# Experts' layer of a fused four-layer kernel: four sets of tile buffers, one buffer for two norms, and a new order of the pieces

## The reference, cut to what matters

```python
q = jnp.einsum('btd,ed->bte', hidden_states, W_q)
sim = jnp.einsum('pbthn,hkpn->pbthk', q, keys)            # 2 x 4 heads x 64 keys
scores_xy, idx_xy = jax.lax.top_k(sim, K)                 # K = 8
all_scores = (sx[..., :, None] + sy[..., None, :]).reshape(b, t, h, K * K)
all_idx = (ix[..., :, None] * nk + iy[..., None, :]).reshape(b, t, h, K * K)
scores, pk = jax.lax.top_k(all_scores, K)
indices = jnp.take_along_axis(all_idx, pk, axis=-1)
w = jax.nn.silu(jnp.einsum('btd,bthkd->bthk', hidden_states, down_embed[indices])
                * jax.nn.softmax(scores, axis=-1))
experts_states = jnp.einsum('bthk,bthkd->btd', w, up_embed[indices])
dense = jnp.einsum('bti,di->btd', jax.nn.silu(jnp.einsum('btd,id->bti', hidden_states, W_up)), W_down)
return dense + experts_states
```

## Time and profile before

| quantity | value |
|---|---|
| median of three runs | 4945.19 us (4938.97 to 4951.75) |
| the profiled execution, its own time | 4949.86 us |
| its span | 4948.5 us |
| experts' layer, from fence to fence | 444.9 to 1078.4 us, 633.5 us |
| busy in its steady part, 513.0 to 1000.7 us | PE 283.4, DVE 406.4, ACT 389.1, POOL 419.0 us of 487.7 |
| first and last `xr` | 551.4 and 1077.7 us |

### The profile page before, as it was taken

How to read it: one execution, slowest core, us unless ns; L and a number is a source line. 1 busy time by engine, 2 the same in 40 slices (tenths; PEclk the granted TensorE clock), 3 DMA queues, 4 the chain that set the end, 5 groups by cost and what they waited for, 6 DMA issues and landing times.

```text
span 4948.5 us, 126756 instructions
## 1 busy us (share of the span) xinstructions
PE 4337.9 (88%) x51520; PEld 3291.1 (67%) x51520; DVE 3905.0 (79%) x6375; ACT 3256.5 (66%) x5035; POOL 3775.0 (76%) x2624
## 2 busy tenths in 40 slices
PE   7885565558867999999999999999999999999997
PEld 5664444446645677777777777777777777777776
DVE  4665888845548888888888888888888888888884
ACT  4664787754434677667676777667676677767675
POOL 1113888853448988888988898889888899888994
PEclk9998778779988999999999999999999999999999
DMA  2000000000001222222222222222222222222222
GB/s 60 2 2 1 1 1 1 1 25 2 2 1 34 52 49 51 66 50 55 51 58 59 56 50 50 63 54 56 50 59 53 53 53 52 62 52 55 49 55 56
DMA packets 120784, 197.93 MB, mean 40 GB/s; under 512 B 66896, under 2 KB 78224, under 8 KB 120080
## 3 DMA queue, kind: packets, MB, share of 16 engines
q1 hardware_dynamic: 120208, 189.82, 15.5%
HBM read 24.12 MB, written 2.10 MB: 5 GB/s over the span
## 4 chain that ended last, share of the span: by engine, by line
PE 65%; ACT 13%; POOL 6%; DVE 6%; issue 5%; DMA 4%; SPq 1%; ACTq 0%; POOLq 0%; DVEq 0%
PE ps L1299 8%; PE ps L1256 7%; PE ps L1249 7%; PE ps L1250 7%; DMA arena<-arena 4%; PE ps L1284 4%; PE ps L1290 3%; PE ps L1291 3%; PE ps L1351 3%; PE ps L1274 3%; PE ps L1310 3%; PE ps L1340 2%; ACT L1385 2%; PE ps L1334 2%; DVE arena L598 2%
## 5 line engine op out<-in xcount | busy, mean ns | idle before, releaser
L1574 POOL TENSOR_TENSOR arena<-arena 128x1024 f32<-128x1024 f32 x384 | 909.5, 2369 | 268.1 <-DVE arena L1474 267.7
L1569 POOL TENSOR_TENSOR arena<-arena 128x32 f32<-128x32 f32 x192 | 1045.0, 5443 | 0.1
L1473 DVE TENSOR_TENSOR arena<-ps,arena 128x1024 f32<-128x1024 f32 x384 | 470.2, 1225 | 344.9 <-ACT arena L1369 344.9
L1369 ACT ACTIVATE arena<-ps 128x1024 f32<-128x1024 f32 x384 | 393.0, 1024 | 386.3 <-PE ps L1250 381.7
L1592 POOL TENSOR_TENSOR arena<-arena 128x1536 f32<-128x1536 f32 x192 | 529.2, 2756 | 113.5 <-DVE arena L1507 113.5
L208 POOL TENSOR_SCALAR arena<-arena 128x2 f32<-128x2 f32 x256 | 87.5, 342 | 624.3 <-DVE arena L202 614.1
L1299 PE MATMUL ps<-arena 96*64 96x64 f32 x12288 | 419.2, 227 | 61.6 <-DMA arena<-arena 59.4
L1474 DVE TENSOR_TENSOR arena<-ps,arena 128x1024 f32<-128x1024 f32 x384 | 466.1, 1214 | 0.0
L1299 PEld LDWEIGHTS ps<-arena 96*64 96x64 f32 x12288 | 393.4, 140 | 91.9 <-issue 84.2
L1256 PEld LDWEIGHTS ps<-arena 128*128 128x128 f32 x3072 | 353.6, 144 | 150.8 <-issue 100.8
L1256 PE MATMUL ps<-arena 128*128 128x128 f32 x3072 | 419.4, 281 | 34.9 <-POOL arena L1579 33.9
(11 more groups left out here) (252 smaller groups left out, 10226.8 us busy)
## 6 DMA issues: line engine op xcount, KB each, us to landing
arena<-arena SPq DMA_DIRECT2D x192, 384.0 KB, 4.3
arena<-arena SPq DMA_DIRECT2D x192, 256.0 KB, 3.7
arena<-arena SPq DMA_DIRECT2D x192, 128.0 KB, 2.3
arena<-in_dWqkv SPq DMA_DIRECT2D x18, 512.0 KB, 3.6
arena<-arena SPq DMA_DIRECT2D x96, 64.0 KB
arena<-arena SPq DMA_DIRECT2D x96, 63.5 KB
arena<-in_dWo SPq DMA_DIRECT2D x6, 512.0 KB, 4.7
arena<-in_x SPq DMA_DIRECT2D x4, 512.0 KB, 7.5
```

The lines of the kernel that those rows point to most:

```text
L1473: dve.tensor_tensor(o1, p.rearrange("p (h e) -> p h e", h=16), bc(cs, 1, 16), ALU.mult)
L1569: pool.tensor_tensor(ss[:, 0:32], ss[:, 32:64], mhalf32, ALU.pow).then_inc(*S.rs.up())
L1574: pool.tensor_tensor(a1[:, half], a1[:, half], T2[:, half], ALU.add).then_inc(*radd[g].up())
```

## The change

- `Tile` exists four times. Batch b uses the sets `2 * (b % 2)` and `2 * (b % 2) + 1`, so a set is written again two batches later. Every wait for the last reader in a tile's buffer changes from the batch before (`if b >= 1: ... at(b)`) to the one before that (`if b >= 2: ... at(b - 1)`).
- `y` is gone. `n1` writes the normed output over `U.h`, and so waits for `h(b)` (which has read it), and `xr` adds `U.h`. Whoever writes `U.h` next is `n0` of three batches later: it waited for `h(b-3)` before and now waits for `xr(b-3)`. What `n1` waited for before (`xr(b-3)`) is dropped.
- `PLACE` has new numbers. Below are its first lines before and after.

```diff
-    Batch = namedtuple("Batch", "st nb h hT up y")
+    Batch = namedtuple("Batch", "st nb h hT up")
...
-                  sb([128, 4, 128])) for _ in range(2)]
+                  sb([128, 4, 128])) for _ in range(4)]
...
-    PLACE = {"n0": 0, "st0": 45, "r0": 54, "hT": 120, "spcA": 193, "piA": 301, "C1A": 370, "mxA": 384, "ixA": 430,
+    PLACE = {"st0": 0, "n0": 38, "hT": 189, "spcA": 304, "spcB": 377, "r0": 416, "piA": 417, "mxA": 511, "h": 521,
...
-            T = tiles[t]
+            T = tiles[2 * (b % 2) + t]
...
             if piece == "n0":
                 X, rs = XR[:, 2 * b:2 * b + 2, :], U.st[2]
                 if b >= NU:
-                    act.wait_ge(*S.h_ps.at(b - NU + 1))
+                    act.wait_ge(*S.xr.at(b - NU + 1))
                 act.wait_ge(*S.r0.at(b + 1))
...
             if piece == "n1":
-                if b >= NU:
-                    act.wait_ge(*S.xr.at(b - NU + 1))
+                act.wait_ge(*S.h_ps.at(b + 1))
                 act.wait_ge(*S.r1.at(b + 1))
                 p, rs = ps("ot", b), U.st[2]
-                act.activation(U.y[:, 0, :], p[:, 0:128], ACT.Identity, bias=U.nb[:, 0:1], scale=rs[:, 0:1])
+                act.activation(U.h[:, 0, :], p[:, 0:128], ACT.Identity, bias=U.nb[:, 0:1], scale=rs[:, 0:1])
...
             if piece in ("spcA", "spcB"):
-                if b >= 1:
-                    act.wait_ge(*gp[t].at(b))
-                    act.wait_ge(*pb[t].at(b))
+                if b >= 2:
+                    act.wait_ge(*gp[t].at(b - 1))
+                    act.wait_ge(*pb[t].at(b - 1))
...
-                pool.tensor_tensor(X, X, U.y, ALU.add).then_inc(*S.xr.up())
+                pool.tensor_tensor(X, X, U.h, ALU.add).then_inc(*S.xr.up())
```

More of the change, by code:

```diff
@@ L781, in phase_b @@
     NU = 3
-    Batch = namedtuple("Batch", "st nb h hT up y")
-    batches = [Batch(stats(C), sb([128, 2]), sb([128, 2, 128]), sb([128, 256]), sb([128, 4, 256]), sb([128, 2, 128]))
+    Batch = namedtuple("Batch", "st nb h hT up")
+    batches = [Batch(stats(C), sb([128, 2]), sb([128, 2, 128]), sb([128, 256]), sb([128, 4, 256]))
                for _ in range(NU)]
@@ new lines, in phase_b @@
+    PLACE = {"st0": 0, "n0": 38, "hT": 189, "spcA": 304, "spcB": 377, "r0": 416, "piA": 417, "mxA": 511, "h": 521,
+             "ixA": 523, "c8A": 576, "mxB": 582, "spA": 595, "mrA": 597, "C1A": 599, "ixB": 632, "C1B": 646,
+             "MA": 705, "nnA": 716, "c8B": 741, "ohA": 796, "mrB": 827, "eqA": 842, "piB": 863, "upc": 865,
+             "trA": 894, "spB": 898, "pcA": 909, "onA": 913, "paA": 922, "paB": 933, "xpA": 940, "txA": 953,
+             "thA": 1012, "xpB": 1014, "eqB": 1178, "pcB": 1227, "mkA": 1229, "up": 1234, "zzB": 1240, "geA": 1249,
+             "nnB": 1295, "trB": 1298, "zzA": 1331, "txB": 1393, "ohB": 1400, "MB": 1407, "sg0A": 1411, "sMA": 1425,
+             "onB": 1438, "pbA": 1461, "gpA": 1472, "sg1A": 1520, "thB": 1521, "mkB": 1596, "pbB": 1603, "geB": 1603,
+             "sg2A": 1646, "sg3A": 1647, "sg0B": 1679, "gpB": 1724, "sg1B": 2016, "atcA": 2103, "sg2B": 2213,
+             "sMB": 2295, "lsA": 2337, "sg3B": 2341, "atcB": 2470, "atA": 2494, "lsB": 2559, "st1": 2823, "n1": 2867,
+             "atB": 3155, "r1": 3250, "xr": 3453, "ot": 3459}
@@ L827, in batch @@
         def batch(piece, b):
-            U, T2 = batches[b % NU], tiles
+            U, T2 = batches[b % NU], (tiles[2 * (b % 2)], tiles[2 * (b % 2) + 1])
             if piece == "h":
@@ L858, in tile @@
         def tile(piece, b, t):
-            U, T = batches[b % NU], tiles[t]
+            U, T = batches[b % NU], tiles[2 * (b % 2) + t]
             if piece in ("spA", "spB"):
@@ L929, in tile @@
             if piece in ("piA", "piB"):
-                if b >= 1:
-                    act.wait_ge(*eq[t].at(b))
-                    act.wait_ge(*pb[t].at(b))
+                if b >= 2:
+                    act.wait_ge(*eq[t].at(b - 1))
+                    act.wait_ge(*pb[t].at(b - 1))
                 act.wait_ge(*ix[t].at(b + 1))
@@ L989, in tile @@
         def tile(piece, b, t):
-            T = tiles[t]
+            T = tiles[2 * (b % 2) + t]
             SIM, PRJ, ey, ex, e8, eC = views(T)
             if piece in ("mxA", "mxB"):
[L993 to L996, removed]
+                if b >= 2:
+                    dve.wait_ge(*pa[t].at(b - 1))
+                    dve.wait_ge(*C1[t].at(b - 1))
+                    dve.wait_ge(*ix[t].at(b - 1))
                 dve.wait_ge(*spc[t].at(b + 1))
```

70 lines of the change are left out of this document (35 added, 35 removed).

## The result

The changed kernel takes 4968.35 us (median of six runs, 4964.66 to 4977.12) against 4942.85 for the kernel before (six runs): ratio 1.0051, 95% interval 1.0040 to 1.0062, so 25 us slower. The forecast was 30 us slower, with a turn (from one `xr` to the next) of 39.8 us.

A forecast was written before the change was run, and what follows sets the result against it. Bound: a chain of data and order waits, no full engine. Four stretches, 19.3 + 10.2 + 3.3 + 7.0 = 39.8 us a turn, +2.3 over 13 batches, +30: 4980 against the profiled execution, median 4975 us, range 4922 to 5008.

The forecast's parts named there:

- What bounds the kernel before: Phase of 633.5 us: a chain of data and order waits through `r1` and `r0`, 37.52 us a turn; more buffers alone remove nothing.
- The loop through the new wait: `n0(b)` waits for `xr(b-3)`, behind `onB` and `nnB`; `mxA` follows: turn 39.8 us for 37.5, +2.3, met by 13 batches.
- Stretch 3: From the start of `nnB` to the end of `xr`, with POOL held by `tr`: 3.3 us, 2.0 from below.
- Stretch 4: From `xr` to `mxA`, through `n0`, `spA` and `spcA`, with PE slow after idling: 7.0 us, 5.3 from below.
- Stretches 1 and 2: DVE from `mxA(b)` to `st0(b+1)`, 19.3 us; then `st0(b+1)` to `nnB(b)`, 10.2 us, with `mkA` waiting for `txA` behind `r1`.
- the wait of 0.6 us for `txB`: Inside `mxA` to `st0`: `mkB` waits for `txB` behind `spB`, `spcB` and the table load, adding 0.6 us to 18.7.
- the end of the phase, set to nothing: Filling and draining of the phase: taken as nothing, give or take 8 us.
- The faster case: Order pays: `r1` ends within 1 us of `st0`, PE at full clock at `spA`; turn 34.4, 4905 us; chance 0.22.
- half-way case: Half of the faster rival's gain: turn 36.3 us or so, time 4930 us; within that rival's chance of 0.22.
- The case of the common ports as the bound: What POOL and DVE exclude each other from sets the turn: within 0.5 us, time within 7 of 4945; chance 0.14.
- the slower rival: `r0` late by one wide piece, so `gpA` holds `xr`: `nnB` to `xr` grows 2.3, turn 42.1, 5005 us; chance 0.14.
- The signs named beforehand: Turn near 40 us, `n0` waiting for `xr`, DVE idle before `mxA`, `mkA` waiting for `txA`, `xr` over 1 us, other phases unchanged.

The follow-up runs named there:

- two kernels that open it in different ways: Changed kernel with the output norm's separate buffer and earlier waits restored: 4915.41 us, ratio 0.9942; changed kernel with `xr` ahead of `r0` on POOL: 4927.19 us, 0.9965.
- the run with four sets: Changed kernel with four sets of statistics buffers in place of three, so `st0(b)` waits for `n1(b-4)`: 4979.74 us, ratio 1.0071.
- the own buffer: Changed kernel, but the output norm has its own buffer in unused `XX`, with the waits of before; same order and tile sets: 4915.41 us, ratio 0.9942.
- the two last kernels with the own buffer: Output norm's separate buffer in the changed kernel, plus four statistics sets and `n1` behind `xpB`: 4915.56 us; or three sets and `r1` ahead of `paA`: 4918.03 us.

## Why the prediction was right, point by point

**What bounds the kernel before:** confirmed in the part that was tried. More buffers in the old order changed nothing (0.9993), and the new order without the new wait shortened the turn to 34.8 us. That the old turn of 37.5 goes through `r1` and `r0` as the chain has it wasn't tried by a run.

**The loop through the new wait:** confirmed by two kernels that open it in different ways, at -4.1 and -3.3 us a turn. The prediction had DVE idle behind `gpA` right, but gave no figure for what the order would be worth without the wait. It is worth 0.58% of 4947, 29 us, and the wait costs the difference of the two ratios, 1.09%, 54 us, PE's lower clock in the changed kernel included.

**Stretch 3,** `nnB` to the end of `xr`: 3.3 us forecast, 744.80 - 741.54 = 3.26 measured. The rows of the trace before held the same sequence, 3.24 us long, and it repeated to within 0.02.

**Stretch 4,** `xr` to `mxA`: 7.0 forecast, 752.05 - 744.80 = 7.25 measured. PE was slow at `spA`, 3.78 us at a granted clock of 0.50, as it had been after idling in the earlier trace rows, where the clock from 733.0 to 737.3 was 0.56. The term matters: in all thirteen turns `spA` took 3.46 to 3.78 us, and after the one of 3.46 the next `n0` came after 38.71 us for 39.03 after the one shown. With the 1.98 us of the fast turns above, this turn would be 37.2 us by estimate (38.95 - 1.80), no longer than before the change, where `spA` is slow too.

**Stretches 1 and 2** were wrong apart and nearly right together. The forecast was 19.3 from `mxA` to `st0` and 10.2 from `st0` to `nnB`, with a wait of 3.6 us for `txA` in the second. Measured are 774.31 - 752.05 = 22.26 and 741.54 - 735.27 = 6.27: 28.5 for 29.5. The same wait for `r1(b-2)` stands one piece earlier, ahead of `st0`, because the statistics have three sets and `st0(b)` must wait for `n1(b-3)`. This step was overlooked in the code. It did no harm to the sum since both waits end with the same `n1`, and the run with four sets shows that they aren't two terms.

What made the 1.0 us too much is mainly `r1`. DVE had come as far as `st0` at 771.55, 19.5 us after `mxA` (forecast 19.3), and `r1` ended 1.8 us behind that (773.37), forecast 2.8. DVE stood idle meanwhile, so no wide piece met any of its four instructions (0.23, 0.71, 0.20, 0.25 us), where the forecast had two of them wait for `eqB`. From the end of `r1` to the end of `txA` it was 3.4 us as forecast, and from `mkA` to `nnB` 3.7 for 4.0. Inside the 19.3, the wait of 0.6 us for `txB` didn't come (`mkB` starts at 756.64, 0.07 us behind the piece ahead of it). As it is written, 3.6 + 1.0 + 1.9 - 4.9 gives 1.6; 0.6 comes out only when the 1.0 us of `spcA`, which ends before `mxA` starts, is taken off as well.

**Sum:** 39.8 us forecast, 38.95 measured. The mechanism held, but the growth of a turn was 1.5 us, two thirds of the 2.3 forecast, and 13 of these are 19 us, not 30. That the whole came to 25 is partly luck: the end of the phase, set to nothing, added some 7 us to the twelve turns. With the own buffer the same stretch takes 79.9 us, so 4.7 of the 7 come with the wait, about the 4.1 us that it costs a turn, and 2.3 with the new order.

**The rivals.** The faster case needed `r1` within 1 us of `st0` and a fast `spA`. The first was met by its words, since `st0` waited for it, and gave no gain: the condition was badly chosen, because it doesn't say where DVE stood meanwhile. The second wasn't met. (Its half-way case should read 36.0 us and 4925; nothing hangs on it.) The case of the common ports as the bound is out at 37.5 us (turns of 35 exist). `xr` held by `gpA`, the slower rival, didn't come about in the changed kernel; it did, at 2.77 us, in the two last kernels with the own buffer, where nobody waits for `xr`.

**The signs named beforehand:** `xr` over 1 us (1.17), `n0` waiting for L1094 (3.2 us), DVE idle ahead of `mxA` (4.5 us) all came; that `mkA` would wait several us for `txA` didn't (0.25 us), for the reason above. That the other phases would keep their times to within 2 us didn't hold behind this phase (7.2 us), where the scatter between traces is as large.

## What to carry to other kernels

When a buffer is shared to save memory, look up where its last reader stands in its engine's order, not how long ago its data was ready: here the data of `xr` had been ready for 8.4 us (`n1` ended at 735.24, `xr` started at 743.63), and the instruction ahead of it made it the last thing that the next batch waited for. Before adding buffers, find a wait for a buffer in the loop; here there was none and only the order paid, and the memory that the order needed lay unused elsewhere. An engine that waits less can lengthen a loop, if its wide instructions then hold the engine that the loop runs through. And look at PE's granted clock in each turn before a difference of 1 or 2 us a turn is put down to the order.

## What was not expected of the hardware

How exactly the holding repeats. In the changed kernel and in the one with the own buffer, `xr` took 1.16 to 1.18 us in fourteen of its sixteen turns (0.72 in the last two). It took 1.70 to 1.72 us when it came ahead of `r0` or when `onB` was held by `ge`, and 2.77 beside `gp`. The time of a POOL instruction goes with the wide DVE instruction that it meets: L1090 or its like, over two columns, has been 0.20, 0.58, 0.88, 1.64, 1.94 and 2.35 us long in these traces.
